# One decoder layer on one core: the exponentials, the copies of turned weights and x1's high part in another order, with round 2, the load of M, the tail and the first rounds

## The reference

```python
# self-attention (8 heads, no softmax)
attn = einsum('bhik,bhjk->bhij', q, k)
out  = einsum('bhik,bhkj->bhij', attn, v)      # then @ w_o.T + b_o
x = layernorm(x + out)                         # x1
# cross-attention, 16 heads of 32, 154 keys
scores = einsum('bhqd,bhkd->bhqk', q, k) / sqrt(32)
scores = where(Mask == 0, -1e9, scores)
attn = softmax(scores);  out = einsum('bhqk,bhkd->bhqd', attn, v)
x = layernorm(x + out @ W_o.T + b_o)           # x2
# feed-forward, x_prev is the row before
xr = mu_r*x + (1-mu_r)*x_prev;  xk = mu_k*x + (1-mu_k)*x_prev
out = sigmoid(xr @ W_r.T) * (square(relu(xk @ W_k.T)) @ W_v.T)
x = layernorm(x + out)                         # y3, the output
```

## Time and profile before

| what | value |
|---|---|
| median of 3 runs | 893.47 us (892.9 to 893.86) |
| time of the profiled execution | 894.21 us |
| its span, first to last instruction | 892.4 us |
| granted TensorE clock, mean | 0.997 of full |
| busy: PE | 851.0 us, 95% |
| busy: DVE | 746.5 us, 84% |
| busy: ACT | 562.4 us, 63% |
| busy: POOL | 519.1 us, 58% |

### The profile page before, as it was taken

How to read it: one execution, slowest core, us unless ns; L and a number is a source line. 1 busy time by engine, 2 the same in 40 slices (tenths; PEclk the granted TensorE clock), 3 DMA queues, 4 the chain that set the end, 5 groups by cost and what they waited for, 6 DMA issues and landing times.

```text
span 892.4 us, 22918 instructions
## 1 busy us (share of the span) xinstructions
PE 851.0 (95%) x8306; PEld 704.5 (79%) x8306; DVE 746.5 (84%) x2049; ACT 562.4 (63%) x1673; POOL 519.1 (58%) x527
## 2 busy tenths in 40 slices
PE   9999999999989999999889999999999999999997
PEld 7877867678778787878778888888888888888786
DVE  6688566567989898989898989898989898987775
ACT  6555425758647676767576767676767676766632
POOL 1036015677857575757576767676766666666520
PEclk9999999999999999999999999999999999999999
DMA  8792020103544544344636353535353535351001
GB/s 281 252 287 69 24 74 26 44 1 127 162 107 131 140 128 140 128 141 127 202 107 159 108 157 111 157 113 157 111 156 113 157 111 156 114 148 36 1 25 47
DMA packets 111698, 107.89 MB, mean 121 GB/s; under 512 B 13794, under 2 KB 86498, under 8 KB 111458
## 3 DMA queue, kind: packets, MB, share of 16 engines
q1 hardware_dynamic: 107986, 99.36, 36.8%
q10 hardware_dynamic: 3600, 7.08, 2.3%
HBM read 64.77 MB, written 40.37 MB: 118 GB/s over the span
## 4 chain that ended last, share of the span: by engine, by line
PE 30%; DVE 30%; issue 10%; POOL 10%; ACT 6%; DMA 1%; SPq 1%; POOLq 0%; DVEq 0%; ACTq 0%
PE dense L97 8%; PE dense L99 8%; PE dense L98 8%; DVE prob L1332 5%; ACT prob L923 4%; DVE k_act_lo L1402 4%; POOL row_inv L1643 3%; POOL prob L1647 3%; DVE stats L1252 3%; DVE mix_k_raw L1390 3%; DVE x_squares L1294 2%; POOL weight L1661 2%; PE turned L1920 2%; DVE mix_r_raw L1379 1%; DVE x L1303 1%
## 5 line engine op out<-in xcount | busy, mean ns | idle before, releaser
L923 ACT ACTIVATE prob<-prob,row_min 128x154 f32<-128x154 f32 x512 | 210.0, 416 | 84.9 <-DVE row_min L1332 84.9
L1643 POOL TENSOR_TENSOR row_inv<-row_sum,minus_one 128x4 f32<-128x4 f32 x128 | 137.6, 1075 | 188.1 <-ACT prob L923 188.1
L1332 DVE CUSTOM_DVE_ANT_0 prob<-scores,mask_add 128x154 f32<-128x154 f32 x512 | 128.5, 310 | 2.3 <-POOL weight L1663 0.4
L1661 POOL TENSOR_TENSOR weight<-prob,row_inv 128x256 f32<-128x256 f32 x152 | 105.5, 714 | 6.0
L923 ACT ACTIVATION_READ_ACCUMULATOR prob<-prob,row_min 128x1 f32 x512 | 98.1, 192 | 0.0
L97 PE MATMUL dense<-xt_hi,cross_wq_hi 128*128 128x256 f32 x256 | 76.3, 298 | 10.2 <-DVE xt_lo L1315 10.0
L1647 POOL TENSOR_TENSOR prob<-prob,row_inv 128x616 f32<-128x616 f32 x52 | 75.0, 1443 | 4.1
L97 PE MATMUL dense<-mix_k_hi,ffn_wk_hi 128*128 128x256 f32 x256 | 75.5, 295 | 0.0
L98 PE MATMUL dense<-xt_lo,cross_wq_hi 128*128 128x256 f32 x256 | 73.9, 289 | 0.0
L99 PE MATMUL dense<-xt_hi,cross_wq_lo 128*128 128x256 f32 x256 | 73.3, 286 | 0.0
L98 PE MATMUL dense<-mix_k_lo,ffn_wk_hi 128*128 128x256 f32 x256 | 72.3, 282 | 0.0
(11 more groups left out here) (286 smaller groups left out, 2650.7 us busy)
## 6 DMA issues: line engine op xcount, KB each, us to landing
weights_scratch<-weight SPq DMA_DIRECT2D x52, 320.0 KB, 2.3
prob_t<-weights_scratch SPq DMA_DIRECT2D x208, 80.0 KB, 2.2
x_scratch<-x_squares SPq DMA_DIRECT2D x52, 256.0 KB, 2.6
x_rows<-x_rows SPq DMA_DIRECT2D x32, 256.0 KB, 4.5
xt_raw<-x_cols SPq DMA_DIRECT2D x16, 512.0 KB, 3.9
out<-gate_then_y SPq DMA_DIRECT2D x15, 512.0 KB, 3.2
xt_raw<-x_scratch SPq DMA_DIRECT2D x52, 128.0 KB, 2.8
x_t<-x_scratch SPq DMA_DIRECT2D x52, 128.0 KB, 3.2
```

What stands on the lines that cost most here:

```text
L923: m = act.activation(keys, keys, ACT.Exp, bias=row_min[:, buf, t, h:h + 1], scale=-1.0, accum_out=row_sum[:, buf, t, h:h + 1])
L1332: m = dve.tensor_tensor_reduce(exp_slot(n, u)[:, i * KEYS:i * KEYS + CTX], s_bank[:, h, t * CTX:(t + 1) * CTX], mask_add[n % 2][:, t, :], ...
L1643: pool.tensor_tensor(inv, row_sum[:, buf, t, :], minus_one[:], ALU.pow).then_inc(*p_inv.up)
L1661: pool.tensor_tensor(to[:, :, spots, :], by_spot[:, :, spots, :], by_side[:, :, w:w + 1].unsqueeze(3).broadcast_to([P, SIDES, 2, SIDE_ROWS ...
```

## The change

It moves calls in the five lists. No operation is added or left out; four subtractions go from one engine to another.

**Loop, ACT.** `x1_high(a)` and `r_gate(e, 1)` stand ahead of `exponentials(n, 3, 0)` (before: behind it). `take_turned(n, 3, 1)` and `take_rest(n, 3, 1)` stand ahead of `exponentials(a, 0, 0)` (before: behind it).

**Loop, DVE.** `v_finish(e, 0)` stands whole ahead of `turn_weights(n, 3)`; before, its first part `v_gated(e, 0)` stood there and its second part `v_sums(e, 0)` behind `blend(f, "k")`.

**Round 2.** `ffn_wr` is loaded one DMA earlier, and `ffn_wv` in round 2 instead of at the end of round 1. `weight_low("ffn_wr")` is split in two halves and `k_low(0, 0)` comes behind `masked_min(2, 2, 1)`. `o_high(1, 3)`, `o_low(1, 3)` and `masked_min(2, 1, 0)` stand earlier, ahead of the loop. POOL makes `r_mix_low(0)` at the end of round 1 instead of at the start of round 2, and `add_bias(3)` behind `weigh(2, 3, 1)` instead of behind `weigh(2, 2, 0)`.

**Load of M (rounds 6 and 7).** SP issues the 1 MB load right behind `fetch_x1`, ahead of `send_weights(n, 2)`, `fetch_x2` and `fetch_weights(n, 2)`; before, behind them. On ACT the four `next_m_high` stand as two pairs. The four `next_m_low` go from DVE to POOL, between `weigh(n, 3, 1)` and `weigh(a, 0, 0)`.

**Tail and first rounds.** ACT takes turned weights of the last group ahead of a ReLU and a square and ahead of `exponentials(LAST, 3, 0)`, PE makes the first half of `r_product(LAST - 1, 1)` ahead of the turning of x2, and in rounds 0 and 1 a few calls change places.

```diff
@@ sp_program @@
                     fetch_weights(n, 0)
+                    if n == 2:
+                        load_weight("ffn_wv")
                     send_weights(n, 1)
...
                     fetch_x1(a)
+                    if a == GPB - 1:
+                        load_batch(batch(a) + 1)
                     send_weights(n, 2)
                     fetch_x2(f)
                     fetch_weights(n, 2)
-                if live(a) and a % GPB == GPB - 1 and a + 1 < NG:
-                    load_batch(batch(a) + 1)
...
                     sp.wait_ge(*fm_mm.at(0))
+                    load_weight("ffn_wr")
                     park(3)
-                    load_weight("ffn_wr")
-                    load_weight("ffn_wv")
@@ act_program, loop @@
                 r_gate(e, 0)
-                exponentials(n, 3, 0)
                 x1_high(a)
                 r_gate(e, 1)
+                exponentials(n, 3, 0)
                 exponentials(n, 3, 1)
                 take_turned(n, 2, 1)
                 take_rest(n, 2, 1)
+                take_q(a, 0)
                 if a == GPB - 1:
                     next_m_high(0)
-                take_q(a, 0)
+                    next_m_high(1)
                 mix_high(f, "k")
                 o_high(n, 2)
                 if a == GPB - 1:
-                    next_m_high(1)
-                exponentials(a, 0, 0)
+                    next_m_high(2)
+                    next_m_high(3)
                 take_turned(n, 3, 1)
                 take_rest(n, 3, 1)
+                exponentials(a, 0, 0)
                 take_q(a, 1)
...
@@ act_program, tail @@
             exponentials(LAST, 2, 0)
+            take_turned(LAST, 1, 0)
+            take_rest(LAST, 1, 0)
             k_relu_half(LAST - 2, 1)
             k_square(LAST - 2, 1)
-            take_turned(LAST, 1, 0)
-            take_rest(LAST, 1, 0)
-            k_high(LAST - 2, 1)
             take_turned(LAST, 1, 1)
             take_rest(LAST, 1, 1)
+            k_high(LAST - 2, 1)
...
@@ dve_program, loop @@
+            masked_min(2, 1, 0)
+            o_low(1, 3)
             for n in range(2, LAST):
                 a, f, e = n + 1, n - 1, n - 2
-                o_low(f, 3)
-                masked_min(n, 1, 0)
+                if e:
+                    o_low(f, 3)
+                    masked_min(n, 1, 0)
...
                 o_finish(f, 0)
-                if n == 2:
-                    weight_low("ffn_wr")
+                if e:
+                    k_low(e, 0)
                 else:
-                    k_low(e, 0)
+                    weight_low("ffn_wr", (0,))
                 o_finish(f, 1)
+                if e == 0:
+                    weight_low("ffn_wr", (1,))
                 turn_weights(n, 1)
-                if n == 2:
-                    k_low(e, 0)
...
                 masked_min(n, 2, 1)
+                if e == 0:
+                    k_low(e, 0)
+                    weight_low("ffn_wv")
                 k_low(e, 1)
-                if n == 2:
-                    weight_low("ffn_wv")
...
                 x1_low(a)
-                v_gated(e, 0)
+                v_finish(e, 0)
                 turn_weights(n, 3)
                 difference(f)
                 blend(f, "k")
-                v_sums(e, 0)
                 o_low(n, 2)
...
-                if a == GPB - 1:
-                    next_m_low(0, 1, 2)
@@ pool_program, loop @@
                 x_low(a)
-                if e == 0:
-                    r_mix_low(e)
...
                 weigh(n, 2, 0)
-                add_bias(a)
+                if e:
+                    add_bias(a)
                 weigh(n, 2, 1)
                 weigh(n, 3, 0)
                 weigh(n, 3, 1)
+                if e == 0:
+                    add_bias(a)
+                if a == GPB - 1:
+                    next_m_low(*range(KT))
                 weigh(a, 0, 0)
```

More of the change, by code:

```diff
@@ L1019, in act_program @@
             take_q(1, 0)
-            exponentials(0, 3, 1)
             u_high(0, 1)
+            u_high(2, 3)
             take_turned(0, 2, 1)
             take_rest(0, 2, 1)
-            u_high(2, 3)
+            exponentials(0, 3, 1)
             o_high(0, 2)
@@ L1073, in act_program @@
             exponentials(2, 0, 0)
+            o_high(1, 3)
             exponentials(2, 0, 1)
@@ L1077, in act_program @@
                 a, f, e = n + 1, n - 1, n - 2
-                o_high(f, 3)
+                if e:
+                    o_high(f, 3)
                 x_high(a)
@@ L1081, in act_program @@
                 k_square(e, 0)
-                exponentials(n, 1, 0)
                 if n == 2:
                     weight_high("ffn_wr")
+                exponentials(n, 1, 0)
                 k_high(e, 0)
@@ L1153, in act_program @@
             turned_x2(LAST - 1, 1)
-            exponentials(LAST, 3, 0)
             take_turned(LAST, 2, 0)
             take_rest(LAST, 2, 0)
+            exponentials(LAST, 3, 0)
             r_gate(LAST - 2, 1)
@@ L1188, in dve_program, with weight_low @@
         def dve_program(dve):
-            def weight_low(name):
-                for i, ks in enumerate(halves_of):
+            def weight_low(name, halves=range(2)):
+                for i in halves:
+                    ks = halves_of[i]
                     dve.wait_ge(*w_hi_ok.at(late.index(name), i + 1))
@@ L1483, in dve_program @@
                     y_finish(a, 0)
+                if n:
+                    y_finish(a, 1)
                 if n > 0:
@@ L1486, in dve_program @@
                 if n:
-                    y_finish(a, 1)
                     normalise(1, a, x1[a % 2])
@@ L1669, in r_mix_low, with next_m_low @@
                                    ALU.subtract).then_inc(*mix_lo["r"].up)
+            def next_m_low(*parts):
+                for k in parts:
+                    pool.wait_ge(*m_hi_ok.at(0, k + 1))
+                    pool.tensor_tensor(m_lo[:, k, :], m_raw[:, k, :], f32(m_hi[:, k, :]), ALU.subtract).then_inc(*m_lo_ok.up)
             def add_bias(n):
@@ L1697, in pool_program @@
                     scale(1, a)
-                if live(n):
+                if n == 0:
                     weigh(n, 2, 0)
-                if n:
+                else:
                     scale(1, a)
                 if n == 1:
+                    weigh(n, 2, 0)
                     add_bias(a)
@@ L1709, in pool_program @@
                     add_bias(a)
+                if live(f):
+                    r_mix_low(f)
                 weigh(a, 0, 0)
@@ L2169, in pe_program @@
             r_product(LAST - 1, 0)
+            r_product(LAST - 1, 1, early)
             x2_turn(LAST, 0)
             x2_turn(LAST, 1)
-            r_product(LAST - 1, 1)
+            r_product(LAST - 1, 1, late_half)
             v_product(LAST - 1, 0)
```

12 lines of the change are left out of this document (1 added, 11 removed).

## The result

The changed kernel takes **900.3 us** (median of 6 runs, 898.34 to 904.29) against 893.36 us (892.9 to 894.63) for the kernel before on the same chip: 1.0078 of it, interval 1.0063 to 1.0093. It is slower by 0.8%. The forecast was 891.6 and faster; the range ended at 898. The profiled execution of the changed kernel took 904.29 us, the longest of the six. The spread is news in itself: six runs of the kernel before lie within 1.7 us, six of the changed one within 6.

The account below looks back on a forecast made before the run. The order of DVE's work was taken to set PE's pace. Round 2 -5.1, steady rounds +4.6, last loop round +0.3, M -0.5 and tail -1.2 summed to -1.9: 891.6 us against 893.47, 8-in-10 range 882 to 898.

Parts of the forecast that it names:

- The circle: Steady rounds: a closed chain from exponentials through x1's send and fetch back to them sets the round; +4.6 us over 11 rounds.
- The rival in which the circle doesn't bind: Steady rounds: x1 lands before the exponentials are due, so PE's waits go; 878.4 us, whole gain 870; chance 0.15.
- +0.42 us: Steady rounds: mean delay per round, from +0.87 in long rounds and -0.03 in short ones.
- half of the rounds short, half long: x1's fetch in steady rounds: six of twelve long (3.8 us), six short (2.9 us).
- 0.90 given back: POOL's `prob` in steady rounds: takes 1.22 instead of 2.12 us, as `x1_low` is over before it begins.
- 0.46 and 0.06 given back: Steady rounds: DVE's idle 0.46 us ahead of `y_finish(a, 1)` absorbs as much delay, a gap on POOL 0.06.
- `v_sums` brings nothing: DVE in steady rounds: moving its 1.5 us ahead of the transpose neither gains nor costs, running while the transpose waits for POOL.
- Round 2: Less DVE holding and no clock loss give -6.2, `v_sums` ahead of the transpose +1.0; taken -5.1, between -3 and -8.
- Load of M: Rounds 6 and 7: PE's waits -3.9, later loads behind M +2.8, port +0.6; -0.5, between -3.6 and +2.
- +2.4: M-load term if the in-order ring makes the loads behind M land up to 5.7 us late, not 2.8.
- Tail: PE's 1.21 us wait at `transposes(LAST, 1, 1)` for the copy of turned weights goes: -1.2, between -1.8 and 0.
- The slower rival: Steady rounds: x1's fetch takes the long time in every round; 899.1 us, or 896.6 with M at -0.5; chance 0.20.

Follow-up runs that it names:

- g1: e4 with x1 read back by one DMA instead of four, leaving the turning of x1 out: 885.71 us.
- e6: Changed kernel with r_gate(e, 1) put back behind exponentials(n, 3, 0), x1_high still ahead of them: 894.19 us, 1.0007 of before.
- e8: Kernel before with only v_sums(e, 0) moved ahead of the transpose of the weights: 919.66 us, 1.0287 of before.
- h1: Changed kernel with its loop ACT edits only in round 2 and the M-load round, v_sums behind the blend everywhere: 889.91 us, 0.9967 of before.
- h2: h1 with the load of M issued behind fetch_x2 and fetch_weights(n, 2) again, as before: 888.76 us, 0.9937.
- e4: Changed kernel with v_sums(e, 0) put back behind blend(f, k) on DVE: 898.06 us, 1.0038 of before.
- e3: Kernel before with only take_turned(n, 3, 1) and take_rest moved ahead of exponentials(a, 0, 0) in the loop: 895.1 us, 1.0018 of before.
- e2: Kernel before with only x1_high(a) and r_gate(e, 1) moved ahead of exponentials(n, 3, 0) in the loop: 915.63 us, 1.023 of before.
- g5: e4 with x1 read back by five DMAs instead of four, the last halved: 899.15 us, 1.0064 of before.
- g6: Kernel before with x1 read back by five DMAs instead of four: 893.7 us, 1.0001 of before.

## Why the prediction was wrong, point by point

**The mechanism was right.** The circle (exponentials, transpose, blend, `o_low`, `y_finish`, send, fetch, `x1_high`) binds, PE's waits went to `o_low`, POOL's `prob` takes 1.22 us, the round changes with the landing. g1 shows it by the landing alone, e6 by ACT's part alone. The rival in which the circle doesn't bind is out.

**Its size was off.** The mean round was forecast at +0.42 us; in the profiled execution it is +1.26. Step by step along the table:

| step | prediction | measured | difference |
|---|---|---|---|
| send to landing, mean | 7.26 (half of the rounds short, half long) | 7.55 | +0.29 |
| landing to exponentials | 1.47 | 1.46 | 0 |
| exponentials to `prob` | 2.90 | 3.11 | +0.21 |
| `prob` to transpose | 1.25 (0.90 given back) | 1.25 | 0 |
| transpose to next send | 32.30 (0.46 and 0.06 given back) | 32.64 | +0.34 |

The failed steps are these. First, "`v_sums` brings nothing". It costs. Beside POOL's `row_inv` it made that 1.29 instead of 1.01 us, and without `x1_high` moved too it holds up the transpose by 1.4 us (e8). The prediction had looked at what the move gains behind the blend and, in round 2, had itself charged +1.0 for the same edit, but in the steady rounds nothing. Second, "DVE's idle 0.46 us takes in as much". Up to `y_finish(a, 1)` it was nearly so: from the transpose to there it took 26.84 us instead of 27.27 (559.47 - 532.63 and the earlier trace rows). But 0.30 of these 0.43 us were lost right behind it. DVE's `var`, two numbers a row, ends when POOL's low part of the mix does, and that ended 29.25 us after the transpose instead of 29.39, so it had moved up by 0.14 only. In the changed kernel (0.76 us to 561.90, beside 561.88) and in the kernel before (0.46 us to 557.93, beside 557.91):

```profile
559.50 2.38 POOL L1664 TENSOR_TENSOR mix_r_lo<-mix_r_raw,mix_r_hi 128x1024 fp32r<-128x1024 f32 x1
...
561.14 0.76 DVE L1255 TENSOR_SCALAR var<-moments 128x2 f32<-128x2 f32 x1
```

```profile
555.54 2.37 POOL L1668 TENSOR_TENSOR mix_r_lo<-mix_r_raw,mix_r_hi 128x1024 fp32r<-128x1024 f32 x1
...
557.47 0.46 DVE L1259 TENSOR_SCALAR var<-moments 128x2 f32<-128x2 f32 x1
```

The prediction knew this port from POOL's side only, as the 0.90 us that come back at `prob`, which they did. Third, the landing: one short and one long round, taken half each, make 7.26 us from send to landing. The ten rounds have a mean of 7.44 in the kernel before (six long ones with 7.84, four short ones with 6.84) and of 7.55 in the changed one.

**Round 2** was forecast at -5.1. From PE's last `values` of round 1 to its last of round 2 it took 45.87 us (215.69 to 261.56) instead of 50.94 (216.34 to 267.28), which is -5.1. At the second send of x1 behind it, which sets the pace, -3.5 was left in the profiled changed kernel, -4.7 in h1 and -2.9 in h2. h1 and h2 have the same code up to there, and 1.4 of the 1.8 us between them stand already ahead of round 2 (214.57 and 215.93): so much a single execution can differ in the first rounds. The mechanism held in the changed kernel: PE's wait of 2.70 us for x1's low part at 254.66 is gone, and with it the stretch at granted 0.50. But of PE's 5.97 us of idle time some came back as `o_low`'s: in the changed kernel a 2.02 at 259.43, which did not lower the clock (in h1 and h2 the waits at this place, 2.24 and 2.59 us, did):

```profile
259.43 0.63 PE L1909 MATMUL turned<-ident,weight 128*128 128x128 f32 x4 [2.02 <-DVE o_t_lo L1345]
```

**Load of M**, forecast -0.5: measured +1.1 against before. Next to an ordinary changed round it is 3.53 longer, next to an ordinary round before 3.71, so -0.2 by itself, in an execution in which M landed late and the clock fell behind the wait. In e4, which differs only by `v_sums`, M landed after 6.12 us, PE waited 1.65 us and the clock stayed: there the stretch took 47.85, 2.19 over an ordinary round, so -1.5. The forecast lies between the two. The direction of the doubt was right. PE's wait for q is gone and a new one stands for weights behind M's load, in the profiled execution this long:

```profile
443.06 1.53 PE L1927 MATMUL turned<-prob_t,v_keys 64*32 64x128 f32 x48 [4.29 <-DMA prob_t<-weights_scratch]
```

The prediction cited the Trainium skill, "DMA: Bandwidth & Descriptors", "Queues, rings and completion order", for a ring that is worked off in order, and +2.4 by it. h1 and h2 differ in this place alone. With M's load ahead (h1) the write of the weights of quarter 2 landed 6.89 us after its issue and behind M, without it (h2) 2.95 us after: the trace agrees with the order, and the delay is 3.9 us. Of it 1.8 us arrive in the M stretch. That is to be held against the 2.8 which the prediction took for this price and the 5.7 that it read from the Trainium skill, and is less than both.

**Tail**, forecast -1.2: nothing came (107.22 against 107.27 us from the last send). The wait of the earlier trace rows is gone, but the last of the waits for `o_low` (1.73 us at 823.00) took its place. In h1, where the chain is not late, the tail is no shorter either (107.49). What holds the end there was not tried.

**The sum.** Forecast -5.1 + 4.6 + 0.3 - 0.5 - 1.2 = -1.9. Measured on the same executions -3.5 + 13.8 (eleven rounds of 1.26) - 0.2 - 0.0 = +10.1. The runs lie at +6.9. The profiled execution was the longest of the six, with M's late landing and one x1 landing of 8.76 us in it; what the other five landings were isn't on record. The slower rival (899.1) was near the number, but named another reason, all landings long; their mean rose by 0.11 us only. Where the forecast failed is that four terms outside the rounds, -6.5 together, brought -3.7, and that three small errors on one chain were multiplied by eleven rounds.

## What to carry to other kernels

A wait on the busiest engine is worth removing only if the chain that ends it gets shorter. Here PE's 1.5 us of waits a round were the difference between its own work and the DVE circle. Moving what PE waited for (e3) moved the wait. So write the circle down as a sum of steps that closes, from one send to the next, and charge each edit to its steps. If an edit puts a DMA's landing into that sum, the DMA's latency and everything that the in-order engine does after it are paid in every round; before, it had been slack. And price each edit alone and with the others: three edits worth +0.25, +2.2 and +2.3 us a round made +1.26 together.

## What the runs showed of the hardware that was not expected

**The clock falls after a single wait of some 2 us, but not each time.** PE waits of 2.03 us (e8) and 2.25 us (e2) were followed by 3.4 us at the 1.2 GHz level in seven and eight of ten rounds, at 1.5 us each. The same waits in the remaining rounds were not, nor was the 2.02 us wait at 259.43 in the changed kernel, nor any of its 1.52 to 1.73 us waits. In the fourteen profiled executions, from 200 us to 850 us, no fall came without a wait of at least 1.98 us that ended as it began or up to 1.6 us before. What decides between two equal waits was not tried. A wait that is split in two may cost less than the same time in one.

**x1's landing has a pattern of four rounds.** From send to landing it takes 6.7 to 7.1 us in two rounds and 7.3 to 8.2 in the next two, with few exceptions, for the same groups in all kernels that fetch x1 in four or five DMAs (5, 6, 9, 10, 13 and 14 are long), also where the rounds last 47 us and not 44.76. So it follows the count, not the time. With one flat DMA (g1) it is nearly gone: 6.0 to 6.6 us for all but one group (7.25). Its cause is open.

**One issue more did not delay the landing.** Four fetches or five, x1 was there after 7.4 us (g5, g6), while one flat DMA of the same bytes took 6.3 (g1).

**Two numbers a row wait like a thousand.** DVE's `shift` on 128x2 took 0.16 us where no POOL subtraction ran and 1.53 us beside one, ending with it to within 0.03 us (e3); `var` does the same. In these kernels what shortened DVE's chain ahead of `var` by 0.43 us gained 0.13 behind it, since POOL's own work had moved by 0.14 only.
